# Features matmuls of two slabs in one block of 32-row tiles, fields read from U, x1 copied instead of y

## The reference

```python
def _cin_layer(x0, x, kernel):
    m = x0.shape[1]
    h_prev = x.shape[1]
    W = kernel.reshape(m, h_prev, kernel.shape[1])
    return jnp.einsum('bmd,bhd,mho->bod', x0, x, W)
x = x0
finals = []
for k in (k1, k2, k3):
    x = _cin_layer(x0, x, k)
    finals.append(jnp.sum(x, axis=-1))
finals = jnp.concatenate(finals, axis=-1)
logit = finals @ kf
```

## Time and profile before

| | us |
|---|---|
| median of the runs shown (three, 314.44 to 315.48) | 315.1 |
| the profiled execution | 314.98 |
| its span on the core | 313.2 |
| PE busy in the span | 298.9 |
| POOL busy | 222.6 |
| DVE busy | 197.9 |
| ACT busy | 183.7 |

### The profile page before, as it was taken

How to read it: one execution, slowest core, us unless ns; L and a number is a source line. 1 busy time by engine, 2 the same in 40 slices (tenths; PEclk the granted TensorE clock), 3 DMA queues, 4 the chain that set the end, 5 groups by cost and what they waited for, 6 DMA issues and landing times.

```text
span 313.2 us, 7674 instructions
## 1 busy us (share of the span) xinstructions
PE 298.9 (95%) x3024; PEld 83.0 (27%) x3026; DVE 197.9 (63%) x217; ACT 183.7 (59%) x195; POOL 222.6 (71%) x131
## 2 busy tenths in 40 slices
PE   7488699999999999999999999999999999999995
PEld 2233122222222222222222222222222222222221
DVE  1486547767665667776665667776665666777631
ACT  2327356766665566776665566776666566676611
POOL 0357468878777777878777777978777777888700
PEclk9769799999999999999999999999999999999999
DMA  6977999999999787888778687888777787610010
GB/s 244 406 326 253 299 377 410 380 361 369 365 339 324 293 300 293 321 329 314 297 284 291 263 296 289 317 333 319 293 296 283 264 295 287 275 36 29 6 36 1
DMA packets 18344, 86.86 MB, mean 277 GB/s; under 512 B 3867, under 2 KB 4123, under 8 KB 9371
## 3 DMA queue, kind: packets, MB, share of 16 engines
q1 hardware_dynamic: 15496, 77.58, 65.0%
q10 hardware_dynamic: 2803, 9.10, 9.9%
q0 software_dynamic: 32, 0.00, 0.0%
HBM read 86.13 MB, written 0.53 MB: 277 GB/s over the span
## 4 chain that ended last, share of the span: by engine, by line
PE 89%; DMA 5%; ACTq 2%; issue 1%; ACT 1%; DVE 1%; POOL 0%
PE acc L547 71%; PE acc L553 11%; PE rot L530 7%; DMA pick<-pick 3%; DMA t_tab<-ts 2%; ACT split L286 0%; ACTq L295 0%; PE acc L561 0%; ACTq L319 0%; DVE xy L471 0%; DVE sums L473 0%; ACT ysb L291 0%; ACTq L323 0%; ACTq L188 0%; POOL split L377 0%
## 5 line engine op out<-in xcount | busy, mean ns | idle before, releaser
L547 PE MATMUL acc<-prod,w 128*32 128x512 f32 x2048 | 228.3, 597 | 0.0
L369 POOL TENSOR_TENSOR prod<-u,v 128x1024 f32<-128x1024 f32 x64 | 152.2, 2400 | 37.3 <-PE acc L553 34.5
L547 PEld LDWEIGHTS acc<-prod,w 128*32 128x32 f32 x2048 | 63.3, 110 | 147.8 <-issue 146.6
L471 DVE TENSOR_TENSOR xy<-acc,ysb 128x512 f32<-128x512 f32 x32 | 22.1, 691 | 94.3 <-ACT ysb L291 94.3
L465 DVE TENSOR_TENSOR prod<-rot,u 128x1024 f32<-128x1024 f32 x64 | 77.8, 1215 | 2.0 <-PE rot L530 2.0
L465 DVE TENSOR_TENSOR prod<-rot,v 128x1024 f32<-128x1024 f32 x64 | 77.8, 1215 | 0.0
L268 ACT ACTIVATE prod<-rot 128x1024 f32<-128x1024 f32 x64 | 65.6, 1026 | 19.4 <-DVE prod L465 17.9
L291 ACT ACTIVATE ysb<-acc,kf 128x512 f32<-128x512 f32 x32 | 22.0, 687 | 78.8 <-PE acc L553 78.8
L272 ACT ACTIVATE feat<-u 128x2048 f32<-128x2048 f32 x32 | 61.0, 1907 | 0.0
L377 POOL TENSOR_TENSOR split<-low,split 128x512 bf16<-128x512 f32 x30 | 34.8, 1161 | 23.7 <-ACT split L286 23.7
L553 PE MATMUL acc<-feat,wf 64*32 64x512 f32 x512 | 35.2, 605 | 2.5 <-issue 2.5
(11 more groups left out here) (36 smaller groups left out, 24.8 us busy)
## 6 DMA issues: line engine op xcount, KB each, us to landing
u<-u_rows SPq DMA_DIRECT2D x31, 1024.0 KB, 4.8
v<-v_rows SPq DMA_DIRECT2D x31, 1024.0 KB, 6.9
xc<-x_chunks SPq DMA_DIRECT2D x32, 256.0 KB, 7.0
feat<-u_rows ACTq DMA_DIRECT2D x32, 256.0 KB, 3.1
u<-k3p SPq DMA_DIRECT2D x2, 512.0 KB, 4.7
u<-u_rows SPq DMA_DIRECT2D x2, 512.0 KB, 8.2
v<-v_rows SPq DMA_DIRECT2D x2, 512.0 KB, 9.3
v<-k2t SPq DMA_DIRECT2D x1, 512.0 KB, 7.2
```

The lines of the kernel that those rows point to most:

```text
L369: nc.gpsimd.tensor_tensor(prod[p][:, UV, pair(half)], us[n][:, pair(half)], vs[n][:, pair(half)], ALU.mult).then_inc(uv_ready, 2)
L471: nc.vector.tensor_tensor(xy[p][:], acc[p][0][:], ysb[p][:], ALU.mult).then_inc(xy_ready, 1)
L547: nc.tensor.matmul(acc[p][h][quad(c), :], w[:, t, h * G:(h + 1) * G], prod[p][:, t, chunk(c)], start=(t == first), stop=False, skip_group_ ...
```

## The change

- `feat` stays the square of `u` on all partitions; `place_fields` and its 32 DMAs go. The linear term reads the fields from `u` itself, with weights `wl` on row groups 2 and 3 (partitions 64 to 95 and 96 to 127), which two small DMAs fill in place of one.
- The features are done once for two slabs, at the end of the step of the even slab: six groups of four matmuls of 32 rows by 32 columns. Row group 0 makes the squares for x1 of this slab and then of the next, row group 2 the squares and the linear term for y of this slab, row group 3 the linear term and the squares for y of the next. The next slab's groups open its accumulators; the odd slab's contraction adds to them and has no features behind it.
- `x1_done` is signalled when x1 is complete, `acc_ready` when y is. ACT copies x1 to SBUF (`take_x1`) where it made `ysb`; DVE adds kf1 to y and multiplies by that copy in one instruction (`scalar_tensor_tensor`).
- `td`, `fold_ps` and `fold` give the weights of y's squares on row groups 2 and 3, with a second small matmul in `fold(1)`.
- `fetch` loads u and v of slab s after `acc_ready` of slab s-4, and `xc` of slab s+1 behind them.

```diff
--- before.py
+++ after.py
+YS = slice(2 * M, P)
-        ysb = [sb(f"ysb_{p}", [P, CHUNK]) for p in range(2)]
+        x1sb = [sb(f"x1sb_{p}", [P, CHUNK]) for p in range(2)]
...
-        td = sb("td", [M, G])
+        td = sb("td", [P, G])
+        wl = sb("wl", [P, G])
...
-        fold_ps = [acc[1][0][2 * M:3 * M, 2 * G:3 * G], acc[1][1][0:M, 2 * G:3 * G]]
+        fold_ps = [acc[1][0][0:M, 2 * G:3 * G], acc[1][1][2 * M:, 2 * G:3 * G]]
...
             def fetch(s, n):
-                if isinstance(s, int) and s < NBUF + 2:
-                    sp.wait_ge(first_split, s - NBUF + 1)
-                else:
-                    sp.wait_ge(split_ready, s - NBUF - 1)
-                load_xc(s, n)
-                read = 4 * (s - NBUF + 1)
-                sp.wait_ge(uv_ready, read)
-                sp.wait_ge(products_ready, read)
-                sp.wait_ge(feat_ready, s - NBUF + 1)
+                sp.wait_ge(acc_ready, s - NBUF + 1)
                 load(s, n)
-
+                if not isinstance(s, int) or s + 1 < SLABS:
+                    load_xc(s + 1, (n + 1) % NBUF)
+
+            sp.wait_ge(first_split, 1)
+            load_xc(NBUF, 0)
             for n in range(NBUF):
                 fetch(NBUF + n, n)
-            with sp.Fori(2, SLABS // NBUF) as it:
+            with sp.Fori(2, SLABS // NBUF - 1) as it:
                 for n in range(NBUF):
                     fetch(NBUF * it + n, n)
+            for n in range(NBUF):
+                fetch(SLABS - NBUF + n, n)
...
-            def place_fields(s, p):
-
-                fields = bass.AP(tensor=u_rows.tensor, offset=s * (P * SLAB), ap=[[SLAB, M], [1, SLAB]])
-                act.wait_ge(feat_ready, s + 1)
-                act.dma_start(feat[p][quad(1), :], fields).then_inc(feat_in[p], 16)
-
...
-            def take_y(s, p):
-                act.wait_ge(acc_ready, s + 1)
+            def take_x1(s, p):
+                act.wait_ge(x1_done, s + 1)
                 wait(act, xy_ready, s - 1)
-                nc.scalar.activation(ysb[p][:], acc[p][1][:], ACT.Identity, bias=kf1[:]).then_inc(y_ready, 1)
+                nc.scalar.copy(x1sb[p][:], acc[p][0][:]).then_inc(x1_ready, 1)
...
-            act.wait_ge(cleared, 2)
+            act.wait_ge(cleared, 1)
...
-            act.wait_ge(cleared, 1)
-            act.dma_start(wf[quad(1), :], ts[M:M + 1, :]).then_inc(lin_in, 16)
+            for group in (2, 3):
+                act.dma_start(wl[quad(group), :], ts[M:M + 1, :]).then_inc(lin_in, 16)
             for half in range(2):
                 act.wait_ge(first_in[half], 32)
             split_mid(2, 0)
             square_fields(0, 0, 0)
-            place_fields(0, 0)
-            act.wait_ge(kf1_in, 16)
...
-                    take_y(s - 1, q)
+                    take_x1(s - 1, q)
...
-                    place_fields(s + 1, q)
...
-            pool.dma_start(td[:], bass.AP(tensor=t_tab.tensor, offset=0,
-                                          ap=[[(WRAP + 1) * G, M], [1, G]])).then_inc(td_in, 16)
+            pool.dma_start(td[YS, :], bass.AP(tensor=t_tab.tensor, offset=0,
+                                          ap=[[0, 2], [(WRAP + 1) * G, M], [1, G]])).then_inc(td_in, 16)
...
             def multiply_xy(s, p):
-                dve.wait_ge(y_ready, s + 1)
+                dve.wait_ge(x1_ready, s + 1)
+                dve.wait_ge(acc_ready, s + 1)
                 wait(dve, sums_ready, s - 1)
-                nc.vector.tensor_tensor(xy[p][:], acc[p][0][:], ysb[p][:], ALU.mult).then_inc(xy_ready, 1)
+                nc.vector.scalar_tensor_tensor(xy[p][:], acc[p][1][:], kf1[:], x1sb[p][:], ALU.add, ALU.mult
+                                               ).then_inc(xy_ready, 1)
...
-            fold_squares(1, quad(0), td[:])
+            fold_squares(1, YS, td[YS, :])
...
-            def contract(s, h, p, tiles, first, count=None):
+            def contract(s, h, p, tiles, first):
                 for t in tiles:
                     if t == UV:
...
                         pe.wait_ge(squares_ready, 2 * s + 2)
                     else:
                         pe.wait_ge(products_ready, 4 * s + (3 if t == UW else 4))
-                    if h == 1 and t == VW and count is not None:
-                        pe.wait_ge(feat_ready, s + 1)
-                        pe.wait_ge(feat_in[p], count)
                     for c in range(CHUNKS):
-                        nc.tensor.matmul(acc[p][h][quad(c), :], w[:, t, h * G:(h + 1) * G], prod[p][:, t, chunk(c)],
-                                         start=(t == first), stop=False, skip_group_check=True)
-
-            def features(p):
-                for h, rows in ((0, slice(2 * M, 4 * M)), (1, slice(0, 2 * M))):
-                    for c in range(CHUNKS):
-                        mm = nc.tensor.matmul(acc[p][h][quad(c), :], wf[rows, :], feat[p][rows, chunk(c)], start=False,
-                                              stop=True, skip_group_check=True)
-                mm.then_inc(acc_ready, 1)
+                        mm = nc.tensor.matmul(acc[p][h][quad(c), :], w[:, t, h * G:(h + 1) * G], prod[p][:, t, chunk(c)],
+                                              start=(t == first), stop=(first is None and t == tiles[-1]),
+                                              skip_group_check=True)
+                return mm
+
+            def feature(h, p, group, weights, source, opens, closes):
+
+                for c in range(CHUNKS):
+                    mm = nc.tensor.matmul(acc[p][h][quad(c), :], weights[quad(group), :], source[quad(group), chunk(c)],
+                                          start=opens, stop=closes, skip_group_check=True)
+                return mm
+
+            def features(p, n):
+
+
+                feature(0, p, 0, wf, feat[p], False, True).then_inc(x1_done, 1)
+                feature(1, p, 2, wf, feat[p], False, False)
+                feature(1, 1 - p, 3, wl, us[n + 1], True, False)
+                feature(0, 1 - p, 0, wf, feat[1 - p], True, False)
+                feature(1, p, 2, wl, us[n], False, True).then_inc(acc_ready, 1)
+                feature(1, 1 - p, 3, wf, feat[1 - p], False, False)
...
             def fold(h):
                 pe.wait_ge(fixed[h], 3)
-                nc.tensor.matmul(fold_ps[h], fixs[:, 4 * P:], w[:, WW, h * G:(h + 1) * G], start=True, stop=True
-                                 ).then_inc(fold_ready[h], 1)
+                for n in range(h + 1):
+                    mm = nc.tensor.matmul(fold_ps[h][quad(n), :], fixs[:, 4 * P:], w[:, WW, h * G:(h + 1) * G],
+                                          start=True, stop=True)
+                mm.then_inc(fold_ready[h], 1)
...
-            pe.wait_ge(feat_ready, 1)
-            pe.wait_ge(feat_in[0], 16)
             for h in range(2):
                 pe.wait_ge(wf_ready[h], 1)
-            pe.wait_ge(lin_in, 16)
-            features(0)
+            pe.wait_ge(lin_in, 32)
+            pe.wait_ge(feat_ready, 2)
+            features(0, 0)
...
                 wait(pe, xy_ready, s - 1)
-                for h in range(2):
-                    contract(s, h, p, (UV, WW, UW, VW), UV, 32 * it + 16 * (n // 2 + 1))
-                features(p)
+                tiles = (UV, WW, UW, VW)
+                if n % 2 == 1:
+                    contract(s, 0, p, tiles, None).then_inc(x1_done, 1)
+                    contract(s, 1, p, tiles, None).then_inc(acc_ready, 1)
+                    return
+                contract(s, 0, p, tiles, UV)
+                contract(s, 1, p, tiles[:-1], UV)
+                pe.wait_ge(feat_ready, s + 2)
+                pe.wait_ge(xy_ready, s)
+                contract(s, 1, p, tiles[-1:], UV)
+                features(p, n)
```

More of the change, by code:

```diff
@@ L145, in cin_kernel @@
         xc_in = [sem(f"xc_in{n}") for n in range(NBUF)]
-        feat_in = [sem(f"feat_in{p}") for p in range(2)]
         t_out, t_in, td_in, lin_in = (
```

9 lines of the change are left out of this document (5 added, 4 removed).

## The result

| | before | after |
|---|---|---|
| median, us (six runs each, on one chip) | 315.29 | 319.71 |
| lowest to highest, us | 314.44 to 317.78 | 318.89 to 321.52 |
| profiled execution, us | 314.98 | 319.73 |
| its span, us | 313.2 | 317.9 |

The change makes the kernel slower: ratio 1.0144, interval 1.0096 to 1.0192. The forecast leaned to slower, with a chance of 0.46; its size was not met: 316.1 was forecast, with a range of 313.6 to 318.0.

A forecast was written before the change was run, and what follows sets the result against it. TensorE, 95% busy, was taken to bound the kernel, with GpSimd 0.7 us short of the slab. Terms -1.82 (start), -1.59 (clock), +5.40 (pairs), -0.86 (end) sum to +1.13 on 314.98: 316.1 us, range 313.6 to 318.0.

The forecast's parts named there:

- The matmuls of the features: TensorE's features block: 24 matmuls in six groups cost two rounds, 1.90 us per pair of slabs, against 2 x 1.02 before.
- rival (d): Features block: the three row groups do not overlap in full, giving 329.8 or 326.7 us; chance 0.07.
- The direct gain of 0.14 per pair: TensorE per pair of slabs, if it never waited: 17.42 us against 17.564, 0.14 less.
- The signal to GpSimd: acc_ready in the fifth group starts GpSimd 2.18 us after the features; TensorE waits 0.29 plus hand-over every second slab.
- The hand-over: GpSimd's split to TensorE's rotation: 0.24 us in the loop, 0.06 written out; with the late signal, 15 pairs cost 5.40.
- The fields' DMA and the start: Start: without the fields' transfer the first features come 1.82 us earlier, at 32.9, though a second small weight transfer costs 0.66.
- The clock: TensorE at the start: the clock stays at 2.4 GHz, regaining the 1.59 us lost before.
- Rival (c): Start: TensorE's clock falls all the same, as idle ahead of the second weight half grows; 317.7 us, chance 0.14.
- Loads, ScalarE, VectorE: Later u and v loads are covered in time; ScalarE's copy and VectorE's new form stay off the path except in the last slab.
- The end: Last slab: from features 30 to the last `xy` 9.08 us instead of 9.94, 0.86 less.
- (a): GpSimd hands over to TensorE fast, 0.06 us everywhere: 2.2 less, 313.9 us; chance 0.20.
- (b): TensorE never waits for GpSimd, so 15 pairs take 261.3 us and the time is 308.5; chance 0.06.

The follow-up runs named there:

- `uv_free` run: Changed kernel with GpSimd's products released by the last reader of tile UV (contraction round 5 of 8), not by acc_ready: 314.79 us, ratio 1.0016.
- the fourth group: Changed kernel with two matmul groups of the features block exchanged, so acc_ready is signalled by the fourth, not the fifth: 317.2 us, ratio 1.0079.
- sixteen matmuls: Changed kernel without the eight matmuls of row group 3, leaving 16 of 24 in the features block: 318.01 us, ratio 1.0109.
- the split last: Changed kernel with TensorE's waits before the rotation reordered to products, squares, then GpSimd's split: 320.06 us, ratio 1.015.

## Why the prediction was wrong in size and right in kind

The leaning to slower came true, but it had only 0.46, with 0.34 for no difference that can be told.

*What bounds the kernel* held. Nothing but GpSimd's chain of 7.77 us, 0.7 short of the slab, came up, and freeing it alone brought the time back (the `uv_free` run).

*The matmuls of the features* is **the step that failed**: "one round more, 1.90", worked out as 1.02 + 0.854 + 0.03 from how two row halves and the bf16 rotation run side by side. It measured 2.17, and through the signal below it enters every pair. I asked whether the row groups overlap (they do: no row shows three rounds) and not how many instructions can be under way. The block of before has 8 float32 matmuls, the contraction's tile shape never more than four side by side, the rotation 12 of bf16; no such block reached 16, so the rows of before did not show a limit, but they also did not carry me to 24. That the cause is a limit on what is under way is the reading that fits the single records and the runs with the fourth group and with sixteen matmuls; no run changes the count alone. My bound 1.87 to 5.29 held this term; the range of the time took only its lower end. "It decides once the block takes over 2.1", I wrote of rival (d); the block was over 2.1 by another mechanism.

The Trainium skill, "TensorE: Matmul & The Clock Gate", The mechanism, says that TensorE has a 64-deep reorder window, through which tiles overlap. Counted in matmuls such a window would have held all 24. Counted in records, four to a float32 matmul, 24 are 96 and the window is full after 16; the trace shows the 17th on time and the 18th held back until the first has ended, so by that count it agrees. No run here shows in another way which of the two is counted.

*The direct gain of 0.14 per pair* was a part of this error: it is a loss of 0.14 (17.70 against 17.564), which the run without waits measures.

*The signal to GpSimd*: mechanism right, size off by the same cause. The fifth group is matmuls 17 to 20, of which all but the first are held: 2.31 instead of 2.18. This +0.13 enters every one of the 15 pairs, 1.95 us: it is the whole excess of the pairs, 1.85, less a little for the hand-over. In the run with sixteen matmuls the signal fell at 2.18 and the pair at 17.95, where I had 17.96. TensorE's wait was smaller than forecast (0.32 against 0.4 to 0.6) for the same reason: its own block had grown by 0.27.

*The hand-over* was right in size: 0.22 in the loop, 0.05 written out, against 0.24 and 0.06. Its composition was not: with the split last it is 0.115 in both, counted to the first weight load as the 0.22 and 0.05 are.

*The fields' DMA and the start*: -1.67 on the comparable stretch, against -1.82. The missing 0.15 lies in the second `wl` transfer: the two held ScalarE 1.54, so the second cost 0.86 and not 0.66. That the first features stood at 34.01 and not 32.9 is for 0.96 the execution's own start (22.65 against 21.69 at the first table transfer). **This is the second step that failed: my sum started the changed kernel where one profiled execution of before had started,** and gave the spread of that start, 21.56 to 22.70 in the variants of the changed kernel, nothing. The runs of before, 314.44 to 315.48, were a hint of it. How the six runs divide between start and loop is open, since only the profiled execution of each kernel has a trace.

*The clock* came as forecast in the profiled execution, at 1.00 from the first features on, and this is in part luck. The profiled execution of before, mean granted clock 0.976, is one that lost it there. Of 78 other executions of before, timed beside the experiments, 39 have a mean of 0.982 or more, and in each of the three groups their median is 0.7 to 1.5 us under that of the rest. So a term of -1.59 against one execution is less against the median; how much less is not shown, as those runs have no trace. Rival (c) did not come, but was nearer than 0.14 says: variants with 2.93, 3.32 and 3.88 us of idle ahead of the second half of the weights lost the clock there, two variants of the changed kernel lost it earlier in the start (at 25.15 and 26.18), and its own two profiles, with 1.13 and 1.14, did not.

*Loads, ScalarE, VectorE* in the steady part: nothing, as forecast. At the start no load held the profiled executions of the changed kernel either. *The end*: -0.57 and not -0.86; 0.27 of the difference is the block again. The 0.33 behind the last `xy` is 0.06 of the new form (0.75 against 0.69) and otherwise the closing steps, which I did not take apart.

*The rivals.* (a), 0.06 everywhere, is false for the loop. (b) is false: TensorE waits in each pair. (d) is false as put, the groups overlap; but it was the nearest to the truth in where it looked. Summed: block and signal 1.95 + 0.27, start 1.11, end of span 0.33, hand-over and rounding -0.1: 3.6, which is what the forecast missed.

## What to carry to other kernels

When work is taken out of one step and put into another, look up who is released by the signal that moves with it, and how much slack that engine has against the step that became shorter, not against the mean. A block of many small matmuls may be priced by the number of instructions under way as well as by rounds; where the trace has no block of that size, keep a term for it in the range. A transfer that seems free at the start must not stand ahead of stores on whose return the weights hang: ahead the first features came 4.3 us later, behind they came 2.5 earlier against the first table transfer, of which the median showed 1.5. And a sum that starts from one profiled execution carries its start and its clock along: compare a second one first.

## What the hardware showed that I had not expected

- In a block of 24 float32 matmuls of 32x32 tiles (four records each) 17 started before the first had ended; further ones followed some 17 ns apart. 24 matmuls in two rounds of three row groups took 2.17 us, 16 on two row groups took 1.87.
- The hand-over from the end of GpSimd's `split` to TensorE's first weight load was 0.05 us where the waits carry constants and the waited one comes first, 0.22 where two waits on a register stand in a row and the first is the late one, 0.115 where the late one stands last.
- 256 KB of fields ahead of two stores of 256 KB raised these from 7.2 to 10.0 us to landing (9.2 in a second kernel); behind them they took 7.5 and 8.2.
- VectorE's `scalar_tensor_tensor` with a per-partition scalar, 128x512 from PSUM and SBUF, took 751 ns, where `tensor_tensor` took 0.69 us; ScalarE's copy 577 ns, where the activation with a bias took 0.69 us.
- The length of one idle stretch of TensorE did not tell whether the clock would fall. Idle of 2.16, 2.46, 2.93, 3.12, 3.32 and 3.88 us, each in another execution, was followed by the lower level (1.2 GHz); idle of 1.14 was not, nor was 2.46 before the rotation at 25.54, 2.62 and 2.85 at the same rotation in two other runs, and 2.84 before the first features.
